# Fillers at the end of TensorE's turn; block sums' low halves to VectorE, two blocks of probabilities' high halves to GpSimdE

## The reference, cut to what matters

```
x = x + xattn(layernorm(x), ctx)        # x: 16 batches x 256 rows x 512
  q = t @ Wq (16 heads of 128); k, v = ctx @ Wk, ctx @ Wv (8 kv heads)
  attn = softmax(mask(q k^T / sqrt(128)));  out = (attn @ v) @ Wo
x = x + ffn(layernorm(x))               # per pair of batches: 4 of 32 experts for each row,
                                        # capacity 128 rows of an expert, plus a shared expert
```

## Time and profile before

| | |
|---|---|
| median of 3 runs | 1707.92 us |
| the profiled execution | 1704.77 us, span 1703.0 us, mean granted TensorE clock 0.987 |
| TensorE matmul busy | 1585.2 us (93%) |
| VectorE busy | 1380.7 us (81%) |
| ScalarE, GpSimdE busy | 1053.2 us (62%), 1035.9 us (61%) |
| DMA | 225.72 MB, mean 133 GB/s |

### The profile page before, as it was taken

How to read it: one execution, slowest core, us unless ns; L and a number is a source line. 1 busy time by engine, 2 the same in 40 slices (tenths; PEclk the granted TensorE clock), 3 DMA queues, 4 the chain that set the end, 5 groups by cost and what they waited for, 6 DMA issues and landing times. The chain is left out here.

```text
span 1703.0 us, 36611 instructions
## 1 busy us (share of the span) xinstructions
PE 1585.2 (93%) x12583; PEld 1186.1 (70%) x12583; DVE 1380.7 (81%) x3723; ACT 1053.2 (62%) x2487; POOL 1035.9 (61%) x1004
## 2 busy tenths in 40 slices
PE   7778999999999999999999999999999899999995
PEld 4556767777777777777777777777776666666662
DVE  7788989998998989899988999898777156766763
ACT  5666676766666666666667666666644156666663
POOL 2766585857667586767768586776766533434332
PEclk9899999999999999999999999999999999999998
DMA  7545774636455454545555454544765558988843
GB/s 208 142 89 110 151 170 101 125 61 134 91 104 104 92 119 76 132 87 117 96 100 107 88 119 77 130 89 100 149 187 198 149 175 228 253 239 237 243 75 50
DMA packets 403751, 225.72 MB, mean 133 GB/s; under 512 B 348769, under 2 KB 360033, under 8 KB 403185
## 3 DMA queue, kind: packets, MB, share of 16 engines
q1 hardware_dynamic: 387104, 197.05, 48.5%
...
q10 hardware_dynamic: 560, 1.05, 0.2%
...
## 5 line engine op out<-in xcount | busy, mean ns | idle before, releaser
L786 POOL TENSOR_TENSOR weight_in<-h_both,weight_in 128x896 f16<-128x896 f32 x128 | 244.0, 1907 | 97.5 <-ACT weight_in L1083 97.5
L1777 PE MATMUL ps_query<-xn_both,arena 128*128 128x256 f16 x1056 | 288.7, 273 | 1.0 <-DMA xn_both<-xn_half 1.0
L1778 PE MATMUL ps_query<-xn_both,arena 128*128 128x256 f16 x1056 | 288.6, 273 | 0.0
L1779 PE MATMUL ps_query<-xn_both,arena 128*128 128x256 f16 x1056 | 288.5, 273 | 0.0
L1083 ACT ACTIVATE weight_in<-h_both 128x896 f16<-128x896 f32 x128 | 121.6, 950 | 260.1 <-POOL h_both L781 256.2
L1436 DVE SCALAR_TENSOR_TENSOR arena<-arena,prob_scale 128x256 f16<-128x256 f32 x512 | 270.8, 569 | 0.6 <-ACT arena L1069 0.6
L1061 ACT ACTIVATE arena<-arena,neg_max 128x256 f32<-128x256 f32 x512 | 253.0, 495 | 25.4 <-DVE neg_max L1411 25.2
L778 POOL TENSOR_TENSOR h_both<-h_both 128x256 f32<-128x256 f32 x128 | 112.4, 878 | 194.8 <-ACT h_both L1076 194.6
L1069 ACT ACTIVATE arena<-arena,prob_scale 128x256 f16<-128x256 f32 x384 | 179.5, 499 | 71.8 <-DVE prob_scale L1420 69.9
L1411 DVE CUSTOM_DVE_ANT_0 arena<-ps_score,mask_add 128x256 f32<-128x256 f32 x512 | 185.6, 418 | 42.4 <-PE ps_score L1779 41.4
L831 POOL DMA_INDIRECT slot_table<-entry,slot_at x128 | 135.9, 1062 | 45.7 <-issue 31.1
...
## 6 DMA issues: line engine op xcount, KB each, us to landing
...
arena<-arena SPq DMA_TRANSPOSE x256, 3.1
```

What stands on the lines that cost most here:

```text
L786: pool.tensor_tensor(l_t.lo, o_full[:, :, :], l_t.hi, ALU.subtract).then_inc(sum_lo, 1)
L1777: pe.matmul(dst, a.hi, b.hi, start=start and n == 0, stop=False, skip_group_check=shared)
L1778: pe.matmul(dst, a.hi, b.lo, start=False, stop=False, skip_group_check=shared)
L1779: m = pe.matmul(dst, a.lo, b.hi, start=False, stop=stop and n == len(pairs) - 1, skip_group_check=shared)
```

## The change

It moves the filler on TensorE from behind `scores(i)` to the end of the turn, behind `project(i-2)`, and its eviction into the next turn, first on ScalarE and behind the maxima on VectorE. In `held` the key of turn i+1 now stands ahead of the filler of turn i. `rank` becomes a filler of j = 0, a turn later than it was. `sums_low` goes from GpSimdE to VectorE. The high halves of cells 2 and 3 go from ScalarE (cell 2) and VectorE (cell 3) to GpSimdE, as a `tensor_scalar` with one scale for each partition. `x_norm` goes from GpSimdE to VectorE (the function is there already, L1281). `x1_norm` is spread over two turns, `combine` stands behind `sums` in the turn ahead of its old one, and the routing steps, the copies of the second layer norm and their DMAs (SyncE) come a turn or two later. Behind the turns `add_shared(1)` comes earlier on GpSimdE (ahead of the last batch's `record`), and late splits 20 and 21 ahead of the gathers. The diff, with `inv_std`'s and other unchanged calls around it and small moves left out:

```diff
@@ -420,20 +420,19 @@
                 return ("value", 1, 1, 1) if j == 0 else ("value", 2, *divmod(j - 1, SB))
+            if b > 1 and j == 0:
+                return ("rank", b - 2)
             if b > 1 and a < B and j in (1, 3, 4, 6):
...
             return None
-
-        def rank_of(b, j):
-            return ("rank", b - 1) if j == KV - 1 and b else None
 
...
             b, j = divmod(i, KV)
+            held += [("key", i + 1)] if i + 1 < TURNS else []
             held += [fill(b, j)] if fill(b, j) else []
-            held += [("key", i + 1)] if i + 1 < TURNS else []
-            held += [rank_of(b, j)] if rank_of(b, j) else []
+        held += [("rank", B - 2)]
         before |= {b_: a_ for a_, b_ in zip(held, held[1:])}
...
@@ -652,7 +651,7 @@
                     load_ctx(b + 2)
-                if j == 4 and b:
+                if j == 5 and b:
                     for t in range(TB):
...
@@ -661,9 +660,9 @@
                     load_x(b + 1)
-                if j == 4 and b:
+                if j == 5 and b:
                     store_xn2(b - 1)
-                if j == 6 and b and LATE.index(b - 1) not in IN_PLACE:
+                if j == 7 and b and LATE.index(b - 1) not in IN_PLACE:
                     keep_x2t(b - 1)
...
@@ -729,24 +728,15 @@
 
-            def x_norm(b):
-                pool.wait_ge(x_rstd, b + 1)
-                pool.wait_ge(xn_lo, TB * b)
-                if b == 2:
-                    pool.wait_ge(weight_lo, JOBS)
-                for t in range(TB):
-                    pool.tensor_scalar(xn_full(b)[:, t, :], x_in[b % 2][:, t, :], mean_var[0][:, t, 0:1],
-                                       rstd[0][:, t:t + 1], ALU.subtract, ALU.mult).then_inc(x_normed, 1)
-
-            def x1_norm(z):
-                pool.wait_ge(x1_rstd, z + 1)
-                if z:
-                    pool.wait_ge(xn2_lo, TB * z)
-                else:
-                    pool.wait_ge(weight_lo, JOBS)
-                for t in range(TB):
-                    pool.tensor_scalar(xn2_full[:, t, :], x1[:, t, :], mean_var[1][:, t, 0:1], rstd[1][:, t:t + 1],
-                                       ALU.subtract, ALU.mult).then_inc(x1_normed, 1)
+            def x1_norm(z, t):
+                if t == 0:
+                    pool.wait_ge(x1_rstd, z + 1)
+                    if z:
+                        pool.wait_ge(xn2_lo, TB * z)
+                    else:
+                        pool.wait_ge(weight_lo, JOBS)
+                pool.tensor_scalar(xn2_full[:, t, :], x1[:, t, :], mean_var[1][:, t, 0:1], rstd[1][:, t:t + 1],
+                                   ALU.subtract, ALU.mult).then_inc(x1_normed, 1)
 
...
@@ -781,9 +771,13 @@
 
-            def sums_low(i):
-                pool.wait_ge(sum_hi, i + 1)
-                pool.tensor_tensor(l_t.lo, o_full[:, :, :], l_t.hi, ALU.subtract).then_inc(sum_lo, 1)
+            def probs_high(i):
+                pool.wait_ge(prob_scaled, i + 1)
+                if i:
+                    pool.wait_ge(turned[PAIR - 1], 16 * i)
+                for c in range(TB, CELLS):
+                    pool.tensor_scalar(p_rows[:, c, 0, :], probs[:, c, :], prob_scale[:, c:c + 1], 1.0, ALU.mult,
+                                       ALU.mult).then_inc(last_hi, 1)
 
...
@@ -862,37 +856,35 @@
                     inv_std(0, a, x_stats, x_rstd, x_normed)
-                if 1 <= i <= KV:
-                    combine(i - 1)
-                if i >= 2:
-                    sums_low(i - 2)
                 if i == 0:
...
                     mask_bias(a)
-                if j == 3 and b:
-                    x1_norm(z)
-                if j == 4 and a < B:
-                    x_norm(a)
-                if j in (1, 2, 5, 6) and b > 1:
-                    record(b - 2, (1, 2, 5, 6).index(j))
+                if j in (3, 4) and b:
+                    x1_norm(z, j - 3)
+                if j in (5, 6, 7) and b > 1:
+                    record(b - 2, j - 5)
+                if j == 0 and b > 2:
+                    record(b - 3, 3)
                 if j == 7 and b + 2 < B:
                     ctx_high(b + 2)
+                probs_high(i)
                 if i:
                     sums(i - 1)
+                if i < KV:
+                    combine(i)
 
...
             late_split(0)
-            sums_low(TURNS - 2)
+            sums(TURNS - 1)
             late_split(1)
-            sums(TURNS - 1)
-            sums_low(TURNS - 1)
+            record(z - 2, 3)
+            for k in (2, 3):
+                late_split(k)
             for part in range(RECORDS // 2):
                 record(z - 1, part)
-            for k in (2, 3):
-                late_split(k)
             inv_std(1, z, x1_stats, x1_rstd, x1_normed)
...
@@ -901,21 +893,21 @@
             add_shared(0)
+            add_shared(1)
             for part in range(RECORDS):
...
                            slot_table.rearrange("(p e) c -> p (e c)", e=E)).then_inc(in_table, 16)
-            add_shared(1)
+            for k in (20, 21):
+                late_split(k)
             pool.wait_ge(in_table, 16)
...
                 gather(e)
-            for k in (20, 21):
-                late_split(k)
             add_shared(2)
...
@@ -1149,29 +1141,29 @@
                 b, j = divmod(i, KV)
+                if i:
+                    filler(fill(*divmod(i - 1, KV)))
                 if i >= 2:
...
                     value_high(ps_fill[1], 0, 0, 0)
-                filler(fill(b, j))
                 exps(i, range(TB, CELLS))
-                if i == TURNS - 1:
-                    piece(0)
                 if i == 0:
...
                     query_high(i + 1)
+                else:
+                    piece(0)
                 probs_high(i, range(0, TB))
...
                     key_high(i + 1)
-                probs_high(i, range(TB, CELLS - 1))
                 if i:
                     head_copy(i - 1)
-                if j == 3 and b:
+                if j == 4 and b:
                     for t in range(TB):
                         xn2_high(b - 1, t)
-                if j == 4 and b + 1 < B:
+                if j == 5 and b + 1 < B:
                     for t in range(TB):
...
@@ -1420,19 +1412,16 @@
 
-            def last_high(i):
-                c = CELLS - 1
-                if i:
-                    dve.wait_ge(turned[PAIR - 1], 16 * i)
-                dve.tensor_scalar(p_rows[:, c, 0, :], probs[:, c, :], prob_scale[:, c:c + 1], None, ALU.mult).then_inc(
-                    last_hi, 1)
+            def sums_low(i):
+                dve.wait_ge(sum_hi, i + 1)
+                dve.tensor_tensor(l_t.lo, o_full[:, :, :], l_t.hi, ALU.subtract).then_inc(sum_lo, 1)
 
...
                 for c in cells:
-                    if c < CELLS - 1:
-                        dve.wait_ge(norm_hi, (CELLS - 1) * i + c + 1)
+                    if c < TB:
+                        dve.wait_ge(norm_hi, TB * i + c + 1)
                     else:
-                        dve.wait_ge(last_hi, i + 1)
+                        dve.wait_ge(last_hi, TB * i + c - TB + 1)
                     dve.scalar_tensor_tensor(p_rows[:, c, 1, :], probs[:, c, :], prob_scale[:, c:c + 1],
...
@@ -1616,61 +1605,65 @@
                 maxima(i)
+                if i:
+                    filler(fill(*divmod(i - 1, KV)))
+                if i >= 2:
+                    sums_low(i - 2)
                 for n in split_amid.get(i, ()):
                     weight_low(n)
-                if j == 0 and b > 1:
+                if j == 1 and b > 1:
                     place(b - 2)
...
                     residual_rest(z)
-                if j == 4 and routed:
-                    for t in range(TB):
-                        xn2_rest(z, t)
-                if j == 5 and a < B:
+                if j == 4 and a < B:
+                    x_norm(a)
+                if j == 6 and a < B:
                     for t in range(TB):
                         xn_rest(a, t)
-                if j == 6 and routed:
+                if j == 7 and routed:
                     choose_2()
...
                     choose_4()
-                if j == 7 and routed:
+                if j == 0 and b > 1:
                     choose_7()
-                    choose_8(z)
-                filler(fill(b, j))
+                    choose_8(b - 2)
                 prob_scales(i)
...
                     query_low(i + 1)
+                else:
+                    piece(0)
                 probs_low(i, range(0, TB))
...
                     key_low(i + 1)
-                last_high(i)
                 probs_low(i, range(TB, CELLS))
...
                     ctx_low(1)
-                if i == TURNS - 1:
-                    piece(0)
-                if j == 0 and b > 1:
-                    pick(score)
-                    choose_9()
-                    choose_10()
-                    choose_11(b - 2)
                 if j == 1 and routed:
...
                         x1_stats_row(z, t)
```

(24 more changed lines are left out.)

4 lines of the change are left out of this document (2 added, 2 removed).

## The result

The changed kernel takes 1700.18 us (median of 6 runs) beside 1707.86 for the kernel before: ratio 0.9956, 95% interval 0.9944 to 0.9968. It is faster by 7.7 us. The forecast was 1660 with a range of 1634 to 1696: right in sign, wrong in size by 40 us, and outside its range. The profiled execution took 1699.66 us, span 1697.9.

What follows compares the result with a forecast made beforehand. TensorE was taken to bound: 71.5 us a batch plus 1.7 of stalls, 73.2. Gains 3 + 4.4 + 3.0 + 12 x 2.3 + 2 + 8 = 48 from 1704.77 gave 1656.8, plus 3.15 to the median: 1660, range 1634 to 1696.

Steps and rivals of the forecast that it cites:

- Fillers at the end of the turn: TensorE: 3.9 us between filler and next key, VectorE's low half done 1 us ahead, so the key's wait goes.
- `sums_low` on VectorE: VectorE, each turn: 1.09 us an instruction, 1.0 start to start, 8.0 us a batch added.
- That is below TensorE's 71.5, but close: Batch: VectorE busy 67.4 us, up to 74.4 if waits stay, against 71.5 for TensorE's turns without the excess.
- What is late next: VectorE late in uneven turns: TensorE stalls 0.7 us in j = 2, 0.8 in j = 4, 0.2 in 7 and 0; together 1.7.
- VectorE's load: Busy time a batch: net 6.3 us of work added, some 7 of waits removed, from 68.1 to 67.4 us.
- GpSimdE's new piece: Sixteen scalings of 256 columns a batch at 1.1 us each, range 0.48 to 2.1; 17.6 us, hidden.
- does this piece disturb VectorE: GpSimdE's scalings beside VectorE's `probs_low`: claimed undisturbed, as two `probs_low` inside such instructions took 0.87 us together.
- rival 4: VectorE is blocked for each new GpSimdE instruction, 10.8 us a batch, and needs 78.2; 1738 us, chance 0.05.
- Batch 0: First batch: the link through `sums_low` goes, the chain to the next weights stays; 3 us gained, bounds -8 and +8.
- Behind the turns: After the last turn: earlier `add_shared(1)` removes TensorE's 5.3 us wait and 2.4 of slow clock; 8 us gained, floor 0.
- rival 2: VectorE becomes the bound, disturbed as much by GpSimdE's new instructions as the old; 1707 us, 1690 half-way, chance 0.12.
- Rival 5: GpSimdE's two scalings in a loop decide from 1.67 us each; at 2.1, 82.4 us a batch, 1797; chance 0.05.

Runs made afterwards that it cites:

- s3: Changed kernel with the high halves of cells 2 and 3 back on ScalarE and VectorE and `sums_low` back on GpSimdE; 1681.53 us.
- s2: Changed kernel with the high halves of cells 2 and 3 back on ScalarE and VectorE, `sums_low` staying on VectorE; 1704.05 us.
- s4: Changed kernel with `sums_low` on VectorE making only 128 of its 896 columns from the second turn on; 1664.86 us.
- s6: s3 with cell 3's high half on ScalarE too, so VectorE has neither `sums_low` nor `last_high`; 1669.36 us.
- s5: Changed kernel with all four high halves made by ScalarE, `sums_low` staying on VectorE; 1687.07 us.
- s10: s6 with routing weights in turn 5, `add_shared(2)` ahead of the gathers, and `combine(i-1)` between `sums_low(i-2)` and `sums(i-1)`; 1635.7 us.
- s12: s10 with `sums_low` on VectorE behind the maxima, as in the changed kernel; 1666.43 us.
- s9: Changed kernel with the routing weights at the end of turn 5 instead of turn 3, and the records waiting for them later; 1684.84 us.
- s7: Changed kernel with GpSimdE's two scalings written with two operands for each partition instead of one and an immediate; 1765.14 us.
- s11: Changed kernel with `add_shared(2)` ahead of the gathers and `combine(i-1)` behind the two scalings, ahead of `sums(i-1)`; 1697.09 us.
- s8: s3 with `x_norm` in turn 5, `add_shared(2)` ahead of the gathers, and `combine` behind `sums` in the turn after; 1695.2 us.

## Why the prediction was wrong

**Fillers at the end of the turn: right.** Three of the four waits of the earlier trace rows went, and turns 1, 3 and 6 came to 9.9, 9.6 and 9.5 us. The fourth, in turn 4, stayed with 1.4 us. s3 shows what the order (with `x_norm`) is worth by itself: 73.7 us a batch.

**`sums_low` on VectorE: the price right, the step wrong.** Its 1.09 us is what the traces have, and the waits under it went (s3 to s2, start to start: 8.1 more for `sums_low`, 6.2 less elsewhere, 1.9 net). What failed is "That is below TensorE's 71.5, but close" together with the stalls of 1.7 us under **What is late next**: I judged load by the batch and sized the lateness of single turns too small. VectorE's slack lies in turns 5 to 7, and lateness is handed on from turn to turn. The measured stalls in the changed kernel, 4.5 us, lie mainly in turn 0 (1.0, forecast 0.1), turn 1 (0.5, forecast none), turn 2 (1.0, forecast 0.7) and turn 4 (1.6, forecast 0.8). (My floor of 71.5 held 0.6 us that the table counts as stall, so the forecast batch of 73.2 stands for 2.3 in the table's terms.)

The two halves of this have different causes. In turns 0 to 2 `sums_low` stands ahead of routing, residual and `prob_scales`; cut to a seventh (s4) it leaves 0.4 of 2.5 us. The pairs s6/s5 and s10/s12 put its price at 1.6 and 2.1 us a batch with VectorE as low as 65 us: 18 to 31 us of time. Turn 4 owes it nothing: with both pieces back its stall is still 1.69 (s3). There it is the routing weights, which the change put at the end of turn 3; VectorE comes 2.3 us late into turn 4, as I had said at the upper end, and my own margin for the filler's wait was 1 us, so I should have charged 1.3 or more and not 0.8. With the weights in turn 5 the stall is 0.03 (s9), and the time 15 us less.

**VectorE's load, 67.4 us: 3.9 short.** The terms, start to start as VectorE's busy time counts them: `sums_low` 8.1 for 8.0 and `x_norm` 0.9 for 1.2 were right. Taking out `last_high` saved 2.3 and not the 2.9 of its group. The waits outside `probs_low` shrank by 7.0, which is the whole forecast. But `probs_low`, where I had counted 2.9 us of waits, grew by 3.4: its group is 20.5 us where it was 17.7 and undisturbed is 14.4 (s5). The waits came from `sums`, which now start under the second pair (7.0 us a batch at the same time before, 11.6 after), and from the quick scalings.

**GpSimdE's new piece: 1.1 us forecast, 0.485 measured.** The row near by form of operand was the wrong one; the lower bound, the same shape with immediates, was right. s7 shows that my row priced the form with two operands for each partition (1.28 us). The step "does this piece disturb VectorE" rested on the same row and fell with it: the slow form leaves VectorE alone, the quick one does not. The Trainium skill, SBUF — State Buffer, section "Who interferes with whom", calls the shared access an exclusive lock for a whole instruction. The quick form and `sums` bear it out in kind, though the pairs shown lost 0.20 and 0.47 us where the two engines ran together for 0.40 and 1.2; the form with two operands (2.50 us, pair 0.87) does not. Its consequence for the time, rival 4's 1738, did not come.

**Batch 0: sign wrong.** 2.9 us longer for 3 shorter, inside the bounds of 8. The link of the earlier trace rows went, as said. The scalings queue behind `combine` instead: with them on ScalarE batch 0 is 99.2 (s5). s11 does not show whether that queue is the cost, since `combine` behind them comes late for ScalarE. The two traces of batch 0 add something that I had left out, first before, then after:

```profile
17.97:117.93 99.96, 75.48 (x541) 54.65 (x542) 83.39 (x171) 67.51 (x149) 61.20 (x62) 0.90 0.54 137
```

```profile
17.88:120.70 102.82, 78.70 (x540) 55.58 (x541) 88.17 (x171) 63.17 (x140) 58.58 (x69) 0.87 0.52 135
```

TensorE is idle as long as before (24.1 us for 24.5), but its matmuls take 3.2 us more, at a mean clock of 0.87 for 0.90: 27.3 us of the batch are at 0.50, where it was 20.5. My 3 us priced waits alone. How the rest divides stays open.

**Behind the turns: wrong.** 8 us forecast, -1.3 measured. `add_shared(1)` was issued some 23 us earlier (1298 for 1321; 6 of them because the turns end earlier) and it did not matter: ScalarE waits for the count `adds_done["s", 1]`, and additions 1 and 2 are counted as one group, so it waits for addition 2, issued at 1328.1 behind the gathers (before, 1330.8). I had named this as the floor ("should the next addition be the one waited for") and not read the table that counts them. s8 and s11 issue addition 2 earlier, and get 9.2 and 9.0 against the same kernel without that move: the price was right, its cause one instruction off.

**Rivals.** The truth lies between the forecast and rival 2 (1707, or 1690 half-way), which had the mechanism closest: new disturbance where the old went. But it named VectorE's sum as the bound, and s9 refutes that: same sum, 15 us less. Rival 5 is what s7 became, at 1.28 us for a scaling and 1765 us, below the 1.67 from which I let it decide: in turn 3 `x1_norm` stands in the same loop and makes the scalings late, which the average turn of that rival hid.
